# Key and value projections of a two-layer block, moved ahead of the attention that reads them

## The reference

```python
x = x + softmax(mask(ln(x) @ ctx.T * scale)) @ ctx          # first attention, one head
x = x + bitlinear(silu(bitlinear(ln(x), w1)) * bitlinear(ln(x), w2), w3)   # hidden 1408
q = ln(x) @ Wq.T + bq ; k = ctx @ Wk.T + bk ; v = ctx @ Wv.T + bv          # 16 heads of 32
s = clip(where(attend, clip(q @ k.T / sqrt(32), -50, 50), -10000), -50, 50)
x = x + layernorm(rs * (softmax(s) @ v @ Wo.T + bo))         # second attention
x = x + (silu(ln(x) @ Wg.T) * (ln(x) @ Wu.T)) @ Wd.T         # integer weights with scales
```

## Time and profile before

| | us |
|---|---|
| median of 3 runs | 628.23 |
| lowest, highest | 620.86, 629.54 |
| the profiled execution, its own time | 627.14 |
| its span, first to last instruction | 625.4 |
| PE busy in the span | 509.3 (81%) |
| DVE busy | 439.9 (70%) |
| ACT busy | 244.8 (39%) |
| POOL busy | 217.3 (35%) |

### The profile page before, as it was taken

How to read it: one execution, slowest core, us unless ns; L and a number is a source line. 1 busy time by engine, 2 the same in 40 slices (tenths; PEclk the granted TensorE clock), 3 DMA queues, 4 the chain that set the end, 5 groups by cost and what they waited for, 6 DMA issues and landing times. The chain is left out here.

```text
span 625.4 us, 10440 instructions
## 1 busy us (share of the span) xinstructions
PE 509.3 (81%) x3595; PEld 386.2 (62%) x3602; DVE 439.9 (70%) x807; ACT 244.8 (39%) x378; POOL 217.3 (35%) x192
## 2 busy tenths in 40 slices
PE   3587745767985597989898989899738868999997
PEld 2455425624442496878888978888736634555796
DVE  5655996667786445887979797978968987555411
ACT  2365412736775543454443444343321233222100
POOL 3103442230000203656566575657658433000000
PEclk9998977987999697999999999999878877999999
DMA  8899815140000026532333332322507040000011
GB/s 275 305 362 375 286 41 189 47 145 28 0 1 0 2 48 144 141 108 64 96 74 92 72 93 70 92 61 55 184 25 269 9 158 28 2 0 0 16 44 59
DMA packets 35671, 63.47 MB, mean 101 GB/s; under 512 B 6833, under 2 KB 28337, under 8 KB 33585
## 3 DMA queue, kind: packets, MB, share of 16 engines
q1 hardware_dynamic: 35632, 62.97, 32.1%
q10 hardware_dynamic: 2, 0.01, 0.0%
HBM read 43.04 MB, written 1.84 MB: 72 GB/s over the span
## 5 line engine op out<-in xcount | busy, mean ns | idle before, releaser
L1307 POOL TENSOR_TENSOR el<-er 128x448 bf16<-128x448 f32 x96 | 114.2, 1215 | 75.7 <-DVE er L1423 75.7
L165 PE MATMUL psum<-kv_p,wk_p 128*128 128x384 f32 x384 | 77.6, 356 | 11.0 <-PEq L626 6.4
L165 PEld LDWEIGHTS psum<-kv_p,wk_p 128*128 128x128 f32 x384 | 70.4, 198 | 13.0 <-issue 9.1
L175 PE MATMUL psum<-wv_p,kv_p 128*128 128x512 f32 x288 | 71.9, 398 | 0.6 <-DVE v_rest_b L201 0.6
L1373 PE MATMUL psum<-vst,e 128*128 128x98 bf16 x384 | 55.8, 213 | 15.6 <-POOL el L1307 6.1
L1423 DVE TENSOR_TENSOR er<-e 128x448 f32<-128x448 f32 x96 | 62.1, 699 | 0.0
L175 PEld LDWEIGHTS psum<-wv_p,kv_p 128*128 128x128 f32 x288 | 53.7, 189 | 11.7 <-issue 0.9
L1373 PE MATMUL psum<-vst,er 128*128 128x98 bf16 x384 | 55.5, 212 | 0.0
L1373 PE MATMUL psum<-vst,el 128*128 128x98 bf16 x384 | 55.5, 212 | 0.0
L1327 ACT ACTIVATE e<-psum 128x448 f32<-128x448 f32 x96 | 44.7, 540 | 24.1 <-PE psum L1358 24.1
L1373 PEld LDWEIGHTS psum<-vst,e 128*128 128x128 bf16 x384 | 38.7, 101 | 23.9 <-issue 10.0
(11 more groups left out here) (199 smaller groups left out, 1004.3 us busy)
## 6 DMA issues: line engine op xcount, KB each, us to landing
kv_raw<-in_ctx_feat SPq DMA_DIRECT2D x16, 768.0 KB, 6.0
kst<-khl_d SPq DMA_DIRECT2D x224, 48.0 KB, 2.0
w_stage<-in_w SPq DMA_DIRECT2D x6, 1408.0 KB, 8.8
cn<-in_ctx_tok SPq DMA_DIRECT2D x8, 768.0 KB, 8.4
w_int<-in_wg SPq DMA_DIRECT2D x2, 1408.0 KB, 8.0
w_int<-in_wu SPq DMA_DIRECT2D x2, 1408.0 KB, 6.2
w_int<-in_wd SPq DMA_DIRECT2D x2, 1408.0 KB, 8.9
qst<-qhl SPq DMA_DIRECT2D x16, 128.0 KB, 2.4
```

The lines of the kernel that those rows point to most:

```text
L165: mm = pe.matmul(psum[:, BK_K + g % 2, 0:TP], wk_p[:, u, k, g * P:(g + 1) * P], kv_p[q][:, v, k, :], start=(k, u, v) == (0, 0, 0), stop=(k ...
L175: mm = pe.matmul(psum[:, BK_V, :], kv_p[q][:, u, k, c * P:(c + 1) * P], wv_p[:, v, k, :], start=(k, u, v) == (0, 0, 0), stop=(k, u, v) == ...
L1307: pool.tensor_tensor(el[q][:, c, 0:4 * S], er[q][:, c, 0:4 * S], halves(er[q][:])[:, c, 0:4 * S], ALU.subtract).then_inc(e_low, 1)
```

## The change: what it does

The key and value products of all 8 elements are computed in A and B: 28 of the 56 products (elements 0, 2, 4, 6) in A, 28 (elements 1, 3, 5, 7) in B. The tables `A_KV` and `B_KV` place them: for each element of A or tile of B, three tuples of product numbers, one for each of three places. A product's results are read by ACT and DVE in two 2 byte parts, for values too (these scaled by 4), and SP writes them to device memory (`kv_spill`). The value columns fall from 98 to 66. In C and D, `kv_fetch` brings the keys of an element, already stacked, with 4 transfers and its values with one; element b+2 is fetched when element b is done. In D nothing is left of the projections. `e`, `er` and `el` have four buffers, PE, ACT and DVE work two groups ahead instead of one, the loops are written out, `clip` and `left` are one instruction each over 3 x 448 numbers, and the mask is a bias of the exponential instead of a bound of the clip. The output weight is loaded and split early in D. Weights of the first feed-forward step go through one staging buffer, so half of the second weight is made ternary in B.

```diff
-UW = 98
+UW = 66
+VS = 4.0
...
+        KV_ORDER = (0, 2, 4, 6, 1, 3, 5, 7)
+        PIECES = (("k", 0), ("k", 1), ("v", 0), ("k", 2), ("v", 1), ("k", 3), ("v", 2))
...
+        def kv_bank(p):
+
+            if p < A_PIECES:
+                return 5 + p % 2
+            return 4 + p % 2 if p < A_PIECES + 8 else 7
...
+        def kv_product(pe, p):
+
+            i, (kind, n) = p // NP, PIECES[p % NP]
+            src = kv_p[kv_slot(i)]
+            pe.wait_ge(ct_lo, kv_split_count(i))
+            pe.wait_ge(proj_lo, 1 if kind == "k" else 2)
+            after(pe, kv_left, p - 1 if kv_bank(p) != 7 else p)
...
+        def kv_spill(sp, p):
+
+            b, (kind, n) = KV_ORDER[p // NP], PIECES[p % NP]
+            sp.wait_ge(kv_left, p + 1)
+            if kind == "k":
+                sp.dma_start(k_scratch[b, n], khl[n][:]).then_inc(k_spilled[n], 16)
+            else:
+                sp.dma_start(v_scratch[b, :, n], vsp[:, n]).then_inc(v_spilled[n], 16)
...
+        def kv_fetch(sp, b, q):
+
+
+            for c in range(4):
+                sp.dma_start(kst[q][32 * c:32 * c + 32].rearrange("d g h t -> d (g h) t"),
+                             k_scratch[b].rearrange("g (h d) u t -> u d (g h) t", h=4)[c % 2]).then_inc(kst_loaded[q], 16)
+            sp.dma_start(vst[q][:], v_scratch[b]).then_inc(vst_loaded[q], 16)
...
+        A_KV = (((), (), (0, 1)), ((2,), (3, 4), (5, 6)), ((7,), (8,), (9, 10)), ((11,), (12,), (13,)),
...
                 add(b)
+                if b == 0:
+                    projection_low(0, wk_p, wk_raw)
+                    dve.wait_ge(consts_loaded, CONSTS)
...
+            ternary_weight(dve, 1, 0)
+            feat_low(dve, B_SLOT[1], B + 2)
...
+            keys_values(range(B_FIRST, B_FIRST + 8))
             turn_input(0)
...
-        e = [at(f"e{q}", [P, TC, EP], F32, R1 + q * 5568) for q in range(2)]
+        e = [at(f"e{r}", [P, TC, EP], F32, ER[r]) for r in range(4)]
...
+            for b in range(B - 2):
+                sp.wait_ge(s_sum, TC * G * (b + 1))
+                sp.wait_ge(pv_sum, G * (b + 1))
+                kv_fetch(sp, b + 2, b % 2)
...
+            for b in range(B):
+                for g in range(G):
+                    m = G * b + g + 2
+                    if m < G * B:
+                        scores(m // G, m // G % 2, m % G)
+                    values(b, b % 2, g)
...
-                for c in range(TC):
-                    dve.wait_ge(e_ready, TC * (G * b + g) + c + 1)
-                    dve.tensor_tensor(er[r][:, c, 0:4 * S], e[r][:, c, 0:4 * S], halves(e[r][:])[:, c, 0:4 * S],
-                                      ALU.subtract).then_inc(e_left, 1)
+                dve.wait_ge(e_ready, G * b + g + 1)
+                dve.tensor_tensor(er[g][:, :, 0:4 * S], e[g][:, :, 0:4 * S], halves(e[g][:])[:, :, 0:4 * S],
+                                  ALU.subtract).then_inc(e_left, 1)
```

More of the change, by code:

```diff
@@ L121, in build @@
[L121 to L140, removed]
@@ new lines, in build @@
+        ct_loaded = [sem(f"ct_loaded{q}") for q in range(3)]
+        ct_hi = sem("ct_hi")
+        ct_lo = sem("ct_lo")
+        proj_loaded = [sem(f"proj_loaded{n}") for n in range(2)]
+        proj_hi = sem("proj_hi")
+        proj_lo = sem("proj_lo")
+        consts_loaded = sem("consts_loaded")
+        CONSTS = 16 * 11
+        kv_sum = sem("kv_sum")
+        kv_hi = sem("kv_hi")
+        kv_left = sem("kv_left")
+        vsp_clear = sem("vsp_clear")
+        vsp_ones = sem("vsp_ones")
+        k_spilled = [sem(f"k_spilled{g}") for g in range(G)]
@@ L163, in k_product @@
             for k in range(KC):
                 for u, v in PARTS:
[L165 to L188, removed]
@@ L749, in rms @@
                 pool.tensor_tensor(s[:, 2:3], s[:, 1:2], neg_half[:, 0:1], ALU.pow).then_inc(h_rms, 1)
-            with pool.Fori(0, TILES // 2) as i:
-                for q in range(2):
-                    rms(2 * i + q, q)
-            rms(TILES - 1, 0)
+            for t in range(TILES):
+                rms(t, t % 2)
         @block.scalar
@@ L812, in turned_hidden, with keys_values, step @@
                                psum_bf[:, B_HT:B_HT + 2, :].rearrange("p a b -> p (a b)")[:, 0:HID], ACT.Copy).then_inc(hqt_ready, 1)
-            def step(t, q, gates, inputs):
+            def keys_values(pieces):
+                for p in pieces:
+                    kv_read_hi(act, p)
+            def step(t, q):
+                gates, inputs = t + 2 < TILES, t + 3 < TILES
+                keys_values(B_KV[t][1])
                 if gates:
@@ L828, in step @@
                     scaled(t + 2, q)
+            act.wait_ge(rnd_ready, 1)
+            keys_values(range(B_FIRST, B_FIRST + 4))
+            normalized(0)
+            normalized(1)
+            keys_values((B_FIRST + 4,))
+            normalized(2)
+            normalized(3)
+            keys_values((B_FIRST + 5,))
+            normalized(4)
+            normalized(5)
+            keys_values((B_FIRST + 6,))
+            normalized(6)
+            sum_weight(act, 2, 0)
+            keys_values((B_FIRST + 7,))
+            sum_weight(act, 2, 1)
             turned_input(0, 0)
@@ L886, in down, with step @@
                 mm.then_inc(down_sum, 1)
-            def step(t, q, gates, inputs):
+            def step(t, q):
+                gates, inputs = t + 2 < TILES, t + 3 < TILES
                 turn_hidden(t)
+                keys_values(B_KV[t][0])
                 if gates:
@@ L909, in _, with keys_values @@
             gate_up(1, 1, 2)
-            tile_steps(pe, step)
+            keys_values((B_MID + 2, B_MID + 3))
+            for t in range(TILES):
+                step(t, t % 2)
         @block.vector
         def _(dve):
+            def keys_values(pieces):
+                for p in pieces:
+                    kv_read_lo(dve, p)
             dve.sem_inc(x2_ready, 1)
+            keys_values((B_FIRST,))
             dve.wait_ge(x1_moved, MOVED)
@@ L1091, in _ @@
         def _(sp):
+            for q in range(2):
+                kv_fetch(sp, q, q)
             queries_stack(sp, 0)
```

754 lines of the change are left out of this document (355 added, 399 removed).

## The result

The changed kernel takes 665.99 us (median of 4 runs, 663.46 to 668.96), the kernel before 628.58 (4 runs, 620.86 to 629.54): a ratio of 1.0625, with a 95% interval of 1.053 to 1.072. It is slower, by about what was predicted (668.1). The profiled execution took 668.96 us, its span is 667.2.

A forecast was written before the change was run, and what follows sets the result against it. PE waits in A and B, and in D, busiest on PE, POOL and DVE stand close behind, taking turns on a shared port. 627.1 + 56.4 (A) + 42 (B) - 57.4 (D) = 668.1 us; range 645 to 690.

The forecast's parts named there:

- D: Longest part before: losing its products, it falls to POOL and DVE taking turns on a shared port, 229.3 to 171.9 us.
- the tiles of B: B behind its front: 20 products cost 49.3 us, partly hidden in PE's waits; +36 us, from +30 to +45.
- The start of A: First products wait for the splits of their weights: first key product at 36.1 us, first value product at 44.0.
- The rest of A: A from 44.0 us on: PE's products and attention work sum to 103.5 us, plus 4.5 of waits.
- The tail: End of A behind the last product: two reads, a ternary step and a split of the context, 5.5 us.
- The front of B: B up to the turn of its first input: more reads and a ternary step delay it, +6 us, from 0 to +9.
- They fill some of PE's waits: Tiles of B: the key and value products there fill 11 us of time in which PE had waited.
- the turns of one group: D: POOL's `low` and DVE's `left`, `clip` and `ctok` add to 5.5 us, less overlap 5.1 per group.
- under 80: Sign of the forecast in D of the changed kernel: PE busy for less than 80 us.
- Rival 1: D: the port does not decide, groups run at DVE's own 3.6 us; kernel 625.6 us; chance 0.12.
- Rival 2: A and B take the products into idle time, +59 us together; kernel 628.7 us; chance 0.06.
- Rival 3: D: the fetch from device memory comes 15 us late for six elements, 90 us; kernel 758 us; chance 0.05.

The follow-up runs named there:

- e7: The changed kernel with each of the 28 key and value products of A cut from 12 matmuls to 1, reads and spills left: 637.0 us, A 129.5.
- e1: The changed kernel without POOL's subtraction `low` in D, the third part of the weights set to zero: 637.1 us, D 133.6.
- e2: The changed kernel without DVE's `clip` in D: 649.1 us, D 148.3.
- e8: The changed kernel with POOL's `low` as one instruction over 1344 numbers instead of three over 448: 688.9 us, D 183.6.
- e3: The changed kernel with `clip` and `left` in D in three pieces of 448 again: 671.4 us, D 169.2.
- e5: The changed kernel fetching keys and values in D only for elements 0 and 1, the other six reusing them: 660.7 us, D 156.8.

## Why the prediction was right

The total was right by luck, as said above. The forecast's own condition was D at 4.7 to 5.6 us per group and the tiles of B at +30 to +45; measured were 4.57 and +47.7, both just outside. What held is the mechanism: A and B grow by about the price of the products, and D falls only to the turns of POOL and DVE.

**The start of A** held: the first key product at 36.91 (36.1 predicted), the first value product at 46.45 (44.0), behind the splits of the two weights. The second is late because the two key products took 5.98 us, where I had 4.4. PE's timeline in A:

```profile
36.91 5.98 PE L156 MATMUL psum<-kv_p,wk_p 128*128 128x384 f32 x24 [3.68 <-DVE wk_p L605]
...
46.45 3.76 PE L158 MATMUL psum<-wv_p,kv_p 128*128 128x512 f32 x10 [3.28 <-issue]
```

**The rest of A** held too: from 46.45 to the end of the last product at about 152.9 are 106.5 us, where the sum of PE's work and 4.5 of waits gave 108 (PE was busy 104.2 and idle 2.3). The tail was 7.0 instead of 5.5. The words beside it were too simple: that DVE's and ACT's work "lies beside" PE's is true of the sum, but e7 shows that this work alone would keep A 28 us above A of before.

**The front of B** held: the first input was turned 28.7 us into B (28 predicted).

**The tiles of B** are the term that was mis-sized: +36 in the prediction, +47.7 measured (135.6 behind the front, 87.9 before). The step that failed is "They fill some of PE's waits", 11 us, and 2 more for a clock that falls less often. Windows of the tiles, first, middle and last, of the changed kernel and then of the kernel before (the cuts do not lie at quite the same instructions):

```profile
188.60:229.70 41.10, 29.99 (x133) 20.45 (x137) 20.48 (x31) 15.64 (x21) 7.28 (x3) 0.81 0.08 29
229.70:307.80 78.10, 75.17 (x410) 51.00 (x415) 48.59 (x88) 41.85 (x55) 2.76 (x5) 0.98 0.14 52
307.80:324.20 16.40, 8.44 (x45) 4.77 (x44) 7.76 (x24) 8.14 (x9) 2.25 (x3) 0.99 0.23 64
```

```profile
123.10:160.00 36.90, 26.51 (x135) 12.82 (x139) 27.17 (x45) 20.52 (x27) 7.45 (x5) 0.86 0.24 77
160.00:200.00 40.00, 31.73 (x198) 16.57 (x201) 30.12 (x62) 26.71 (x32) 2.75 (x5) 1.00 0.00 0
200.00:211.00 11.00, 4.16 (x15) 1.36 (x12) 3.78 (x13) 4.08 (x4) 2.63 (x5) 0.71 0.00 1
```

PE's idle time in the tiles was 25.5 us before and 22.0 after: 3.5 us were filled, not 11. Its busy time grew by 51.2, where 49.3 less 2 had been priced; the clock gave nothing back. 51.2 - 3.5 are the 47.7. The products did fill the middle tiles, where PE is now idle for 2.9 of 78.1 us (8.3 of 40.0 before), but neither the first tiles (11.1 of 41.1, and 10.4 of 36.9 before) nor the end. PE's timeline in B, where the front ends at 188.6:

```profile
173.70 4.58 PE L158 MATMUL psum<-wv_p,kv_p 128*128 128x512 f32 x12 [2.83 <-DVE vsp L179]
...
188.63 0.59 PE L880 MATMUL psum<-ident_bf,xq 128*128 128x128 bf16 x4 [3.38 <-DVE khl L176]
...
205.54 3.04 PE L158 MATMUL psum<-wv_p,kv_p 128*128 128x512 f32 x12 [2.29 <-DVE khl L176]
...
215.44 4.18 PE L156 MATMUL psum<-kv_p,wk_p 128*128 128x384 f32 x12 [3.47 <-DVE vsp L179]
221.03 4.81 PE L158 MATMUL psum<-wv_p,kv_p 128*128 128x512 f32 x12 [1.41 <-DVE khl L176]
...
271.24 4.20 PE L158 MATMUL psum<-wv_p,kv_p 128*128 128x512 f32 x12 [2.55 <-DVE khl L176]
```

The old waits for `hid` and `hq` mostly went (14.0 us before, 2.4 after), as said, but at seven places in B, 16.8 us in all, PE now waits for the read of an earlier product, which DVE does in its own order. Four of the products behind such a wait then ran 1.2 to 1.9 us longer than the 2.25 and 2.96 of their kind, at a granted clock of 0.50 to 0.68; the one at 205.54, behind a wait of 2.29, ran at 1.00. I had priced the new reads as work beside PE's, and not asked in which queue they stand.

**D** held in its mechanism and not in its size. The port decides (e1, e2 and e8), the sum of turns changes little with their pieces (e3), the fetch is hidden (e5), the two engines' handing over limits the group. The term that was mis-sized is the turns of one group, 4.57 and not 5.1. Beside POOL's own 2.78 I had 0.89 for `clip`, 1.54 for `left` and 0.29 for `ctok`, less 0.4 of overlap: 2.32. They cost POOL 0.38 to 0.59, 1.31 and 0.05; by the mean 4.57 - 2.78 = 1.79, of which 0.28 is POOL's own idle time between the first `low` and the last. From the first to the last values the sum had 158.1 - 4 + 2.3 = 156.4 us, and it took 141.8; that is the miss. PE busy "under 80" was wrong (90.8): at the clock of 0.72 its value matmuls started up to 55 ns apart, where I had priced none above 44; it cost nothing, since PE waits for POOL. The first values came 10.5 us into D (9.7), the end 6.0 behind the last (5.8).

**The rivals.** Rival 1 (groups at DVE's own 3.6, decided below 3.8) fell with the 4.57 of the changed kernel; even without `low` (e1) it is at 3.86. Rival 2 (A and B fill idle time) fell with the windows: together they grew by 113, not by 59. Rival 3 fell with e5.

## What to carry to other kernels

Moving work to a part with idle time on its engine gains only if the whole chain of that work fits there: each product needed PE, then ACT, then DVE and a bank, and the idle time of PE in B was itself spent waiting for DVE, 14 us of it for `hid` and `hq`. Before taking an engine's work out of a long part, find what paces the part without it: here the removal of 112 us of PE's work from D gave 71, because POOL and DVE took turns behind it. And where two engines exclude one another, a short instruction on one side is worth more than fewer starts: three pieces of 0.93 us beat one of 2.43 by 25 us over 32 groups.

## What the runs showed of the hardware that was not expected

A `clip` (one input and one output in SBUF, 4-byte, 1.08 us) keeps a POOL subtraction that begins beside it waiting for only 0.4 to 0.6 us of its length; where the subtraction ran first, it is `clip` that waits, and takes up to 1.85 us. A `left` (two inputs in SBUF, 1.56 us) keeps POOL waiting to within 0.14 of its end. The Trainium skill (SBUF — State Buffer, "Who interferes with whom") calls the port pair an exclusive lock, held for the whole instruction. For `left` and `ctok` the traces agree to within 0.15 us, with the waits of 1.31 and 1.9 us above. For `clip`, one input, the section's lock holds in a two-port mode, which no row here names; the traces show a wait, but of less than its whole length. The addition of the values' parts, which reads PSUM, lay wholly beside a `low` (393.62 to 394.03) and took 0.41; in e1, without any `low`, its mean is 0.42.
